# A transformer block on one core: another order of TensorE's work in the FFN steps and in the first five attention units

## The reference

```python
def reference(x, W_Q, W_K, W_V, W_O, b_Q, b_K, b_V, b_O, gate_w, up_w, down_w, gate_s, up_s, down_s):
    xn = layernorm(x)                                  # over the last axis
    q, k, v = (einsum('bpd,hde->bphe', xn, W) + b for W, b in ((W_Q, b_Q), (W_K, b_K), (W_V, b_V)))
    scores = where(causal, einsum('bqhe,bkhe->bhqk', q, k) / sqrt(128), -1e5)      # 16 heads of 128
    z = einsum('bkhe,bhqk->bqhe', v, softmax(scores))
    s = einsum('bqhe,hed->bqd', z, W_O) + b_O
    hidden = silu((xn @ gate_w.T) * gate_s) * ((xn @ up_w.T) * up_s)               # 1408 wide
    g = silu((hidden @ down_w.T) * down_s)
    return x + s * g
```

## Time and profile before

| what | us |
|---|---|
| median of 3 runs (lowest, highest) | 1109.03 (1108.92, 1110.69) |
| the profiled execution, its own time | 1107.56 |
| span of its trace, first to last instruction | 1105.4 |
| PE busy | 1068.8 (97%) |
| DVE, ACT, POOL busy | 811.4, 736.9, 182.4 |

### The profile page before, as it was taken

One profiled execution on the slowest core, in us unless ns is written; L12 is line 12 of the kernel. 1 busy time (PEld: TensorE's weight loads), 2 busy tenths in 40 slices (PEclk: granted clock), 3 DMA queues, 4 the chain that ended last, 5 costly groups with the idle time before them and its releaser, 6 DMA issues.

```text
span 1105.4 us, 21538 instructions
## 1 busy us (share of the span) xinstructions
PE 1068.8 (97%) x7452; PEld 705.1 (64%) x7452; DVE 811.4 (73%) x2011; ACT 736.9 (67%) x1832; POOL 182.4 (16%) x189
## 2 busy tenths in 40 slices
PE   6999998998899999999999999999999999999998
PEld 3434443445677777777777777777677777777764
DVE  7766876774777777777777777777777777776876
ACT  6745556654677776777777677777666666666662
POOL 1000000000401122121312212122100000144433
PEclk9999999998999999999999999999999999999999
DMA  7335666677568878977897696869667567868765
GB/s 277 135 76 155 159 184 184 183 243 220 119 177 188 206 184 212 226 177 179 229 226 197 168 278 159 204 173 259 184 139 188 136 142 183 225 169 232 213 167 162
DMA packets 318533, 207.68 MB, mean 188 GB/s; under 512 B 251872, under 2 KB 284640, under 8 KB 317920
## 3 DMA queue, kind: packets, MB, share of 16 engines
q1 hardware_dynamic: 295872, 179.64, 64.8%
q10 hardware_dynamic: 19200, 15.73, 4.5%
q0 software_dynamic: 3360, 11.01, 2.8%
HBM read 109.87 MB, written 34.60 MB: 131 GB/s over the span
## 4 chain that ended last, share of the span: by engine, by line
PE 84%; DVE 6%; ACT 5%; DMA 3%; issue 2%; DVEq 0%; SPq 0%; ACTq 0%
PE bank L720 75%; PE bank L879 9%; ACT arena L1234 1%; DMA split_v<-w_out 1%; DMA arena<-arena 1%; ACT arena L1248 1%; DVE arena L1442 1%; DVE arena L1319 1%; DVE arena L1437 1%; DMA split_qk<-w_out 0%; DVE w_out L1335 0%; ACT arena L1113 0%; DVE arena L1380 0%; ACT w_out L1074 0%; PE bank L731 0%
## 5 line engine op out<-in xcount | busy, mean ns | idle before, releaser
L720 PE MATMUL bank<-XT,arena 128*128 128x256 f16 (+2 forms) x1872 | 316.6, 314 | 4.7 <-issue 4.1
L720 PE MATMUL bank<-arena 128*128 128x512 f16 (+1 forms) x1124 | 276.3, 379 | 4.9 <-DVE arena L1442 4.3
L720 PEld LDWEIGHTS bank<-XT,arena 128*128 128x128 f16 (+1 forms) x1872 | 179.3, 98 | 114.7 <-issue 9.3
L1234 ACT ACTIVATE arena<-bank,neg_max 128x512 f32<-128x512 f32 (+3 forms) x256 | 132.8, 525 | 138.4 <-DVE neg_max L1589 138.3
L720 PE MATMUL bank<-ST,arena 128*128 128x256 f16 x1536 | 200.0, 273 | 3.6 <-issue 2.4
L720 PEld LDWEIGHTS bank<-arena 128*128 128x128 f16 x1124 | 107.5, 98 | 116.2 <-issue 15.4
L720 PEld LDWEIGHTS bank<-ST,arena 128*128 128x128 f16 x1536 | 148.4, 98 | 27.7 <-ACT arena L1191 3.3
L1589 DVE CUSTOM_DVE_ANT_0 bank<-bank,mask 128x512 f32<-128x512 f32 (+3 forms) x256 | 118.0, 515 | 20.9 <-PE bank L720 20.7
L1606 DVE SCALAR_TENSOR_TENSOR arena<-arena,inv_sum 128x512 f16<-128x512 f32 (+3 forms) x256 | 127.1, 558 | 7.5 <-ACT arena L1248 5.4
L1248 ACT ACTIVATE arena<-arena,inv_sum 128x512 f16<-128x512 f32 (+3 forms) x256 | 122.3, 557 | 0.0
L879 PE MATMUL bank<-arena,V 128*128 128x512 f16 x756 | 113.1, 299 | 1.2 <-DMA arena<-arena 0.7
(11 more groups left out here) (123 smaller groups left out, 1560.8 us busy)
## 6 DMA issues: line engine op xcount, KB each, us to landing
arena<-split_qk SPq DMA_DIRECT2D x64, 896.0 KB, 5.2
w_in<-attn_w_dram SPq DMA_DIRECT2D x64, 256.0 KB, 4.3
split_qk<-w_out ACTq DMA_DIRECT2D x28, 256.0 KB, 3.6
arena<-ffn_w_dram SPq DMA_DIRECT2D x8, 768.0 KB, 4.9
arena<-x_dram SPq DMA_DIRECT2D x20, 256.0 KB, 3.9
parked_silu<-arena ACTq DMA_DIRECT2D x4, 1024.0 KB, 4.5
arena<-split_o SPq DMA_DIRECT2D x4, 1024.0 KB, 6.0
split_qk<-w_out SPq DMA_DIRECT2D x13, 256.0 KB, 3.5
```

The lines of the kernel that those rows point to most:

```text
L720: mm = nc.tensor.matmul(out, stationary(a, k), moving(b, k), start=first and n == 0 and i == 0, stop=last and n == len(tiles) - 1 and i == ...
L1234: e = nc.scalar.activation(probs[:, at:at + width], SC[b_][:, col:col + width], ACT.Exp, bias=neg_max[:, i:i + 1], scale=-1.0, accum_out=r ...
```

## The change

In the FFN a step on PE runs gate, up, and then all four blocks of the last step's product down, where it ran gate, blocks 0 and 1 down, up, blocks 2 and 3 down. DVE waits for `ht_lo` before it writes `hidden` again, which the old order implied. At the end of a chunk the four scalings and the four silus come in one piece behind the halves of `hidden`. In units 0 to 4 the scores begin with two passes of the two widest tiles that read the keys' high half only, and wait for `k_lo` behind them; in odd ones of these units DVE's `sum_v` comes two operations later. In all units of the loop the wait for `v_sum` now stands ahead of the last score tile alone.

```diff
@@ PE, step
                 project_ffn(GATE, 0, c, m, exact).then_inc(gate_mm, 1)
-                pe.wait_ge(ht_lo, n)
-                down(*before, (0, 1), first, final, exact)
                 if before_up:
                     before_up()
                 pe.wait_ge(hidden_ok, n)
                 project_ffn(UP, 1, c, m, exact).then_inc(up_mm, 1)
                 if after_up:
                     after_up()
-                down(*before, (2, 3), first, final, exact)
+                pe.wait_ge(ht_lo, n)
+                down(*before, range(TT), first, final, exact)
@@ PE, scores
+            def score_tile(g, passes=PASSES, first=True, last=True):
+                i, b_, col, _ = SCORE_TILES[g]
+                width = (i + 1) * P
+                mm = product(SC[b_][:, col:col + width], lambda a, _: Q[a][:, i * P:(i + 1) * P],
+                             lambda b, _: K[b][:, 0:width], [0], first, last, passes)
+                if last and i != 2:
+                    mm.then_inc(score_mm, 1)
+
+            def scores(n, keys_hi_first=False, v_sums=0):
+
+                if n > 0:
+                    pe.wait_ge(exp_ok, 2 * n)
+                pe.wait_ge(q_lo, 2 * (n + 1))
+                if keys_hi_first:
+                    pe.wait_ge(k_hi, 2 * (n + 1))
+                    for g in (0, 1):
+                        score_tile(g, ((0, 0), (1, 0)), True, False)
+                pe.wait_ge(k_lo, 2 * (n + 1))
+                for g in (0, 1):
+                    if keys_hi_first:
+                        score_tile(g, ((0, 1),), False, True)
+                    else:
+                        score_tile(g)
+                score_tile(2)
+                if v_sums:
+                    pe.wait_ge(v_sum, v_sums)
+                score_tile(3)
@@ PE, unit
-                if v:
-                    pe.wait_ge(v_sum, 3 * p + (1 if opens else 3))
-                pe.wait_ge(exp_ok, 2 * n)
-                pe.wait_ge(q_lo, 2 * (n + 1))
-                pe.wait_ge(k_lo, 2 * (n + 1))
-                scores()
+                scores(n, keys_hi_first=not out, v_sums=3 * p + (1 if opens else 3) if v else 0)
@@ ACT, step
-                if down_of is not None:
-                    silu_down(down_of, (0, 1))
                 act.wait_ge(hidden_ok, n + 1)
                 nc.scalar.activation(HT[0][:, slot], hidden, ACT.Copy).then_inc(ht_hi, 1)
                 if down_of is not None:
-                    silu_down(down_of, (2, 3))
+                    silu_down(down_of, range(TT))
                     park(down_of)
@@ DVE, step
-                if down_of is not None:
-                    scale_down(down_of, (0, 1))
+                if n > 0:
+                    dve.wait_ge(ht_lo, n)
...
                 if down_of is not None:
-                    scale_down(down_of, (2, 3))
+                    scale_down(down_of, range(TT))
@@ DVE, unit
-                if v:
+                late = opens and u < LAG
+                if v and not late:
                     sum_v(p, 0 if opens else 1)
                 second_key_lo(n)
                 second_query_sum(n)
+                if v and late:
+                    sum_v(p, 0)
                 second_query_lo(n)
```

More of the change, by code:

```diff
@@ L1012, in _ @@
             pe.wait_ge(v_lo, 2)
-            pe.wait_ge(q_lo, 2)
-            pe.wait_ge(k_lo, 2)
-            scores()
+            scores(0)
             pe.wait_ge(down_scaled, TT * B)
```

7 lines of the change are left out of this document (removed).

## The result

The changed kernel took 1102.03 us by the median of 8 runs (1100.28 to 1107.1), beside 1108.49 of the kernel before on the same chip: a ratio of 0.9945, 95% interval 0.9928 to 0.9962, 6.1 us less (4.2 to 8.0). Against the forecast of 1104.3 and its range of 1101.0 to 1107.4 the sign and the range hold; the gain is 1.4 us larger than my sum. The profiled execution took 1101.67 (span 1099.5), 5.9 under the profiled one of before.

A forecast was written before the change was run, and what follows sets the result against it. PE was taken as the bound, busy 1068.8 us of 1105.4. FFN terms of 4.2 us and units of 0.5 made 4.7 us, taken from the median of 1109.03 to give 1104.3; range 1101.0 to 1107.4.

The forecast's parts named there:

- Step 2 of chunk 0, 0.7: FFN, chunk 0: DVE's flag for step 2 comes earlier, so PE gains 0.7 us; 0.3 to 0.9.
- The stall before step 9 stays: FFN, chunk 0: PE's wait for DVE's flag before step 9's gate product remains, so no gain there.
- Chunk 1 and the turned rows, 0.8: Two low-half delays in chunk 1 go, 0.4 us; PE's wait for turned rows at chunk 2's start goes, 0.4.
- The boundary, 0.1 lost: Start of chunk 2: step 1's silu ends later and delays step 2's gate product by 0.1 us.
- Chunk 2, 1.3: Chunk 2, steps 4 to 9: late operations stay fixed to step 4's gate product; PE gains 1.3 us, between 0 and 3.9.
- Chunk 3, 1.2: FFN, chunk 3: delays of 0.80, 0.29 and 0.13 us go, 1.2 us gained.
- The added self-wait, 0: FFN: DVE's wait for its own `ht_lo` before `hidden` costs 0 us; at the other end 1.8.
- The seam "otherwise the same": Between FFN and units: the seam comes 4 us earlier and is otherwise unchanged.
- Units, 0.5: Units 0 to 4: PE gains 3.1 us at the scores but keeps 0.5 us; between 0.2 and 3.1.
- The rivals: Five other outcomes: all waits go 0.10, stores pace 0.16, clock at the seam 0.12, stall for a stall 0.06, slower 0.04.
- slower: Units 0 to 4: the clock falls in PE's idle times, 2.2 us each, giving 1113.1 us; chance 0.04.
- The stores do pace chunks 2 and 3: Rival: stores set the time in chunks 2 and 3, leaving 2.4 us of gain, 1106.6 us; chance 0.16.

The follow-up runs named there:

- e1: The kernel before with the FFN part of the change alone, scores and units as before: 1103.81 us, ratio 0.9954.
- e11: The changed kernel with `sum_v` back in front of the second key's low half: 69.32 us between scores of heads 0 and 6, against 69.18 changed.
- e12: The changed kernel itself run once more, on another chip: 1104.84 us, ratio 0.9952 to the kernel before.
- e10: The kernel before with DVE's flag of step 9 of chunk 0 set early, nothing else: 1110.10 us, ratio 1.0017.
- e2: The kernel before with the units part of the change alone, FFN as before: 1107.88 us, ratio 0.9990.
- e4: The changed kernel without the keys' high half first in units 0 to 4: 69.87 us between scores of heads 0 and 6, against 69.18 changed.
- e6: The changed kernel with the flag of step 9 of chunk 0 set early and ACT's last store issued late: 1100.26 us, ratio 0.9918.

## Why the prediction was right or wrong, point by point

The sum of 4.7 met 6.1, and that it came so near is in part luck. In the profiled execution the FFN's four chunks gained 3.6 us for the forecast 4.2 (less 0.5, then 1.0, 2.0 and 1.1), the seam 0.4 for 0, the units 1.25 for 0.5, and the rest 1.1 for 0, less 0.4 of a later start: one term too high, three too low.

- *Step 2 of chunk 0, 0.7.* Right for step 2: the gate product comes 13.63 behind the first one instead of 14.53, 0.9, where 0.7 was forecast with 0.9 at most. Chunk 0 as a whole kept it only where the clock didn't fall: without the shift of 0.86 it gained 0.7 and 0.6 in e1 and e11, and lost 0.5 to 0.7 in the three profiles with the fall.
- *"The stall before step 9 stays".* Right that it stays, wrong to end there. I said that the wait of 0.3 for L1442 lies inside the same stretch. It did, and joined to the rest it made one idle time of 2.1 us where there had been 0.48 and, behind the two halves of the product down and the up product between them, 1.64. In half of the profiles the clock fell behind it, 1.6 us. My rivals looked for a fall in the units and for one less at the seam, and never at the longest idle time of chunk 0, which the change made longer. The Trainium skill (TensorE: Matmul & The Clock Gate, Part 1) says that the number of matmuls which one kernel runs at the lower level at its start varies from run to run with the gate's phase. Six profiles with like idle times and three falls fit that, in the middle of a kernel; no run tells the phase.
- *Chunk 1 and the turned rows, 0.8.* Right by the size: 1.0 in the first profile, 0.2 to 1.0 in ten of eleven profiles of the new order. In the eleventh (e12) it was 1.3 worse: PE waited 1.35 us for the turned rows, and 0.57 for `hidden`. I had not forecast that the turned rows would be late before chunk 3 too (0.2 to 0.6 in all eleven), and its last sign of being wrong, transposes that land later, did show there.
- *The boundary, 0.1 lost.* Right: the gate product of step 2 of chunk 2 is delayed by 0.13.
- *Chunk 2, 1.3.* The waits at up of steps 7 and 8 were forecast as 0.5 and 1.1 and came as 0.49 and 1.13. That the gate product of step 6 stays 11.1 behind that of step 4 failed: 10.36 in this execution, and the product of step 9 27.6 behind, not 28.5. ACT's late split came 8.84 behind the product of step 4, not 9.71, though it waited 1.70 for its store and not 1.47: it does not keep its distance from that product. Over the eleven profiles the two distances are 10.4 to 11.5 and 27.6 to 28.9, in the middle 10.75 and 28.3, so the forecast holds better for them than for the first profile. The whole chunk gained 0.4 to 2.0, 1.3 in the middle, against 0.2 + 1.3.
- *Chunk 3, 1.2.* Right: 1.1, in nine of eleven to the floor.
- *The added self-wait, 0.* Right: at ten steps of 5.18 in chunk 3 there is no room for it on the path, so the time holds the 0 and not the 1.8. That says nothing of its cost on DVE itself, which no run here isolates; the rule of the Trainium skill behind the forecast's 0 isn't tested by it.
- *The seam "otherwise the same".* Nearly true of the first profile (0.4 shorter, and the clock 0.50 behind it as before), false in general. The changed order moves ACT's last store ahead of PE's need for code by 0.4 to 1.6 us, where it was 0.16 before (0.27 in e10, and behind it in e2). In e1 and e4 the seam took 2.6 and 1.35 us more than before, without the shift of 0.86. The second idle time, with the packet behind the store, rose by 2.4 and 1.5 us there, the first by 1.4 and 1.2, and less work at the lower clock took some back.
- *Units, 0.5.* This is the term that was mis-sized most: 1.25. The failed step is "The chain moves by 0.2 in unit 0, 0.3 with unit 1, 0.3, 0.5 and 0.5". Measured behind the scores at the seam, the first maxima came 0, 0.38, 0.67, 0.94 and 1.24 us earlier in units 0 to 4. Unit 2 before, then units 1 and 2 after (the earlier trace rows has 302.45 for unit 1 before; the scores at the seam stood at 278.09 before and 274.51 after):

```profile
314.55 0.69 DVE L1589 CUSTOM_DVE_ANT_0 bank<-bank,mask 128x512 f32<-128x512 f32 x1
```
```profile
298.49 0.69 DVE L1599 CUSTOM_DVE_ANT_0 bank<-bank,mask 128x512 f32<-128x512 f32 x1
...
310.30 0.69 DVE L1599 CUSTOM_DVE_ANT_0 bank<-bank,mask 128x512 f32<-128x512 f32 x1
```

  Unit 0 gained nothing where I wrote 0.2; the odd units 0.38 and 0.27 for my 0.1 and 0.2; units 2 and 4 gained 0.29 and 0.30 where I wrote 0. With the old score order (e4) they gain 0. So in these units the maxima do follow PE's earlier products, by 0.3 of the 0.5 to 0.7 that its scores come earlier. Which of ACT's copies carries it I didn't isolate. Units 2 and 4 took 11.1 us, where I had written 11.2 to 11.7; of the new waits that I named one came, 0.2 us for ACT's copies in unit 3, beside 0.3 in front of `weigh_v` in unit 0.
- *The rest.* This term I put at nothing. 1.1 of the profiled 5.9 lies near 454 us, between the scores of heads 14 and 16, where PE waited 0.67 for the transposed probabilities before and not at all after:

```profile
454.01 1.19 PE L879 MATMUL bank<-arena,V 128*128 128x512 f16 x7 [0.67 <-DMA arena<-arena]
```
```profile
448.35 1.79 PE L898 MATMUL bank<-arena,V 128*128 128x512 f16 x12
```

  The wait is 0.77 in e2, 0.51 in e1, 0.35 in e10. Of the ten profiles with both parts of the change nine have none and gain 1.0 us there, while e6 waits 1.15. So it may well come from the change, though neither part alone brings it (0.1 and 0.2 us in e2 and e1). The cause stays open. Waits for other DMAs later in the kernel take some of it back, 0.8 to 1.1 us in e4 and e12.
- *The rivals.* None of them came: in the changed kernel's first profile the clock at the seam was 0.50 again. The sum under *slower* had a slip that changes nothing: three falls of 2.2 us make 6.6, so the third already turns the gain of 4.7 into a loss of 1.9, inside what a measurement tells apart. The stores do pace chunks 2 and 3 in part: the late splits of ACT are there in each profile.

## What to carry to other kernels

Before an order is changed that joins two idle times of PE into one, look at what the clock does behind the longer one, and at who delivers late there: here one engine's flag stood behind 4 us of DVE's work that PE's next product didn't need, and moving it took 1.6 to 2.8 us out of chunk 0, as much as any term of the change. Where PE leaves a branch, count its code as a transfer, and keep large stores from being issued just before it. When executions of one code differ by 5 us, cut several profiles at the same marks before giving a gain to a term.

## What the runs showed of the hardware that I had not expected

- A code packet of 16 KB that PE needed at once started at once when a 1 MB store had been issued up to 1.0 us before (seven profiles), and 1.8 and 2.6 us late when it had been issued 1.4 and 1.6 us before (e4 and e1); PE went on 1.2 to 1.5 us behind the packet's end.
- Behind idle times of 1.94 to 2.00 us the granted clock fell to the level of 1.2 GHz in three of six profiles; behind the 1.5 us in brackets of the kernel before, in the same step, it was 1.00 (two profiles).
- The units repeat to 0.05 us over the nine profiles that share their code, the DMA-fed parts only to 1 to 3 us.
